# Graph attention on one core: vector engine and DMAs turn ten heads of twelve, values one graph later

## The reference

```python
q, k, v = (split_heads(x @ W + b) for W, b in ((Wq, bq), (Wk, bk), (Wv, bv)))
scores = einsum('bhqd,bhkd->bhqk', q, k) / sqrt(32) + beta * adj
probs = softmax(where(adj > 0, scores, -9e15))
x = layernorm(x + merge_heads(einsum('bhqk,bhkd->bhqd', probs, v)))
```

## Time and profile before

| | before |
|---|---|
| median of 3 runs | 678.68 us |
| the profiled execution, its own time | 678.75 us |
| its span, first to last instruction | 677.0 us |
| PE busy | 635.4 us, 94% |
| PE weight loads busy | 514.5 us, 76% |
| DVE busy | 597.7 us, 88% |
| ACT busy | 576.0 us, 85% |
| POOL busy | 406.9 us, 60% |
| DMA queue of SP | 100.37 MB, 57.9% of 16 engines |
| mean granted TensorE clock | 0.993 |

### The profile page before, as it was taken

The page is one execution under the profiler, slowest core; times in us unless marked ns, Lnnn a source line. Parts: engine busy times, 40 slices in busy tenths (PEclk is TensorE's granted clock), DMA queues, the critical chain, the costliest instruction groups (busy, mean ns, idle before and its releaser), DMA issues. The chain is left out here.

```text
span 677.0 us, 21340 instructions
## 1 busy us (share of the span) xinstructions
PE 635.4 (94%) x6304; PEld 514.5 (76%) x6304; DVE 597.7 (88%) x2385; ACT 576.0 (85%) x2024; POOL 406.9 (60%) x642
## 2 busy tenths in 40 slices
PE   5899999999999999999999999999999999999981
PEld 5788877787878787878777777888787878787850
DVE  3898899988999898989898989898989998898974
ACT  4799888889898889898888888888989888988881
POOL 3413266766566775566775556676556676566743
PEclk9999999999999999999999999999999999999997
DMA  8065556567656557755557755556765556765441
GB/s 254 4 148 142 139 136 166 126 164 187 172 143 162 137 140 189 185 150 153 145 122 187 187 155 151 153 119 177 188 172 144 154 127 157 189 168 144 114 101 70
DMA packets 68226, 101.93 MB, mean 151 GB/s; under 512 B 10512, under 2 KB 36368, under 8 KB 68112
## 3 DMA queue, kind: packets, MB, share of 16 engines
q1 hardware_dynamic: 67024, 100.37, 57.9%
q10 hardware_dynamic: 1088, 0.20, 0.2%
HBM read 22.94 MB, written 12.58 MB: 52 GB/s over the span
## 5 line engine op out<-in xcount | busy, mean ns | idle before, releaser
L433 ACT ACTIVATE probs<-neg_scores,neg_max 128x256 f32<-128x256 f32 x768 | 382.4, 504 | 4.4 <-DVE neg_max L515 2.9
L515 DVE CUSTOM_DVE_ANT_0 neg_scores<-s_bank,bias_sb 128x256 f32<-128x256 f32 x768 | 282.3, 416 | 54.2 <-ACT probs L433 45.0
L554 DVE STREAM_TRANSPOSE blocks<-probs 128x512 f32<-128x512 f32 x248 | 171.3, 700 | 0.0
L433 ACT ACTIVATION_READ_ACCUMULATOR probs<-neg_scores,neg_max 128x1 f32 x768 | 149.8, 195 | 0.0
L326 PE MATMUL j_bank<-xt_high,w_high 128*128 128x256 f32 x576 | 115.6, 309 | 1.9 <-ACT w_high L465 1.5
L399 PE MATMUL s_bank<-qk 32*128 32x256 f32 x1536 | 110.0, 399 | 5.4 <-DVE neg_max L515 3.7
L399 PEld LDWEIGHTS s_bank<-qk 32*128 32x128 f32 x1536 | 72.6, 184 | 46.7 <-ACT v_sb L452 28.1
L760 POOL TENSOR_SCALAR o_sb<-y_sb,rstd,shift 128x384 f32<-128x384 f32 x60 | 99.3, 1662 | 9.6 <-POOL shift L755 9.6
L326 PE MATMUL j_bank<-xt_high,w_low 128*128 128x256 f32 x576 | 99.5, 280 | 0.0
L326 PE MATMUL j_bank<-xt_low,w_high 128*128 128x256 f32 x576 | 99.2, 280 | 0.0
L369 PE MATMUL j_bank<-ident,probs 128*128 128x128 f32 x544 | 84.1, 278 | 13.9 <-issue 12.8
(11 more groups left out here) (56 smaller groups left out, 899.2 us busy)
## 6 DMA issues: line engine op xcount, KB each, us to landing
shuffled<-blocks SPq DMA_DIRECT2D x496, 128.0 KB, 3.1
x_sb<-in_x_dram SPq DMA_DIRECT2D x32, 384.0 KB, 3.3
out_dram<-o_sb SPq DMA_DIRECT2D x30, 384.0 KB, 4.3
adj_sb<-in_adj_dram SPq DMA_DIRECT2D x32, 256.0 KB, 3.7
out_dram<-o_sb SPq DMA_DIRECT2D x4, 192.0 KB, 2.1
blocks<-in_L_gnn_Wq_dram SPq DMA_DIRECT2D x1, 576.0 KB, 5.8
blocks<-in_L_gnn_Wk_dram SPq DMA_DIRECT2D x1, 576.0 KB, 8.2
blocks<-in_L_gnn_Wv_dram SPq DMA_DIRECT2D x1, 576.0 KB, 9.6
```

Of the source, the lines that this page charges most:

```text
L433: nc.scalar.activation(probs[:, (T * s + t) % (T * NX), :], neg_scores[:, (T * s + t) % (T * NH), :], ACT.Exp, bias=neg_max[:, n % 2, t, h ...
L515: nc.vector.tensor_tensor_reduce(neg_scores[:, (T * s + t) % (T * NH), :], s_bank[h % J][:, t * N:(t + 1) * N], bias_sb[:, n % 2, t, :], - ...
L554: nc.vector.transpose(blocks[:, n % 2, :, h, :, :].rearrange("p k t q -> p t k q"), probs[:, slot:slot + T, :].rearrange("p t (k q) -> p t ...
```

## The change

Heads 8 and 9 go the way of DVE and DMAs too (HV = 10), so that PE turns heads 10 and 11 only. Now each O needs the shuffle, so O 2 of a graph also moves one graph later, as O 0 and O 1 were. The DMAs remain 16 per graph, each a quarter larger. ACT takes K instead of DVE. The jobs are spread anew over the steps. Three buffers go, to make room: beta*adj is written over the adjacency, the residual sum over `att`, and the rings `probs` and `probs_t` shrink. The moments move from step 8 to step 10, `seed` from 9 to 11; on POOL `residual(n + 1)` goes ahead of `add_residual(n - 2)`; on SP `load_x` goes last. In the last graph all heads are still turned by PE; ten of them are put into the free half of `shuffled` once O 2 of graph 29 has read it.

```diff
-    NX = 6
+    NX = 5
-    HV = 8
+    HV = 10
-    NP = 8
+    NP = 4
@@ jobs_of, graphs 0 to 30 @@
                 0: (("O", 1, n - 2),),
-                1: (("K", 0, n + 1),),
+                1: (("X", 0, n + 2), ("K", 0, n + 1)),
                 2: (("G", 1, n - 2), ("Q", 0, n + 1)),
-                3: (("V", 0, n + 1),),
-                4: (("O", 2, n - 1),),
-                5: (("X", 0, n + 2), ("K", 1, n + 1)),
-                6: (("G", 2, n - 1), ("Q", 1, n + 1)),
-                7: (("X", 1, n + 2), ("Q", 2, n + 1)),
+                3: (("K", 1, n + 1),),
+                4: (("O", 2, n - 2),),
+                5: (("X", 1, n + 2), ("Q", 1, n + 1)),
+                6: (("G", 2, n - 2), ("Q", 2, n + 1)),
+                7: (("V", 0, n + 1),),
                 8: (("O", 0, n - 1),),
                 9: (("X", 2, n + 2), ("K", 2, n + 1)),
                 10: (("G", 0, n - 1),),
...
@@ jobs_of, the last graph @@
-                1: (("O", 2, n - 1),),
+                1: (("O", 2, n - 2),),
-                3: (("G", 2, n - 1),),
+                3: (("G", 2, n - 2),),
...
-                11: (("O", 1, n),),
+                11: (("O", 2, n - 1), ("O", 1, n)),
...
-    last_jobs = (("G", 1, B - 1), ("O", 2, B - 1), ("G", 2, B - 1))
+    last_jobs = (("G", 2, B - 2), ("G", 1, B - 1), ("O", 2, B - 1), ("G", 2, B - 1))
...
     def on_act(job):
-        return job[0] in "QVXO" or (job[0] == "T" and (job[2] < B - 1 or job[1] % 2 == 1))
+        return job[0] in "QKVXO" or (job[0] == "T" and (job[2] < B - 1 or job[1] % 2 == 1))
@@ place_of @@
+            if n == B - 1 and h < HV:
+                half = shuffled[:, n % 2, :, :, :, :, :].rearrange("p k a h t q -> p (k a h t q)")
+                return (half[:, h * T * N:(h + 1) * T * N].rearrange("p (k q) -> p k q", k=T), ("O", 2, n - 2))
@@ sync, shuffle @@
                 if n >= 2:
-                    wait_job(sp, ("O", 1, n - 2))
+                    wait_job(sp, ("O", 2, n - 2))
@@ sync, the loop @@
                 shuffle(n)
+                if n + 3 < B:
+                    load_adj(n + 3)
+                if n >= 3:
+                    store(n - 3)
                 if n + 4 < B:
                     load_x(n + 4)
-                if n + 3 < B:
-                    load_adj(n + 3)
-                if n >= 2:
-                    store(n - 2)
+            store(B - 4)
@@ scalar, before the loop @@
-            for h in range(2):
-                exps(h)
-            for job in second_jobs:
+            exps(0)
+            for job in second_jobs[:2]:
+                take(job)
+            exps(1)
+            for job in second_jobs[2:]:
                 take(job)
@@ vector, take G @@
-                    wait(dve, y_ready, n - 1)
+                    if n < B - 1:
+                        wait(dve, normed, T * (n - 1))
@@ vector, the loop @@
-                    if h == 8 and n >= 2:
+                    if h == 10 and n >= 2:
                         for t in range(T):
                             moments(n - 2, t)
                         gather_moments(n - 2)
-                    if h == 9 and n >= 2:
+                    if h == 11 and n >= 2:
                         seed(n - 2)
@@ gpsimd @@
             def bias(n):
-                pool.wait_ge(adj_in[n % 2], (n // 2 + 1) * DMA)
-                wait(pool, bias_ready, n)
-                take_wait()
-                nc.gpsimd.tensor_scalar(adj_beta[:, :, :], adj_sb[:, n % 2, :, :], 0.0, beta_col[:, 0:1],
+                pool.wait_ge(not_edge_ready, n + 1)
+                nc.gpsimd.tensor_scalar(adj_sb[:, n % 2, :, :], adj_sb[:, n % 2, :, :], 0.0, beta_col[:, 0:1],
                                         ALU.max, ALU.mult).then_inc(adj_beta_ready, 1)
...
             def add_residual(n):
                 pool.wait_ge(taken_v, max(dve_taken[place["G", g, n] + 1] for g in range(G)))
                 pool.wait_ge(res_ready, n + 1)
-                wait(pool, normed, T * n)
-                nc.gpsimd.tensor_tensor(y_sb[:, :, :], att[:, n % 2, :, :], x_sb[:, n % XB, :, :], ALU.add).then_inc(y_ready, 1)
+                nc.gpsimd.tensor_tensor(att[:, n % 2, :, :], att[:, n % 2, :, :], x_sb[:, n % XB, :, :], ALU.add).then_inc(y_ready, 1)
@@ gpsimd, the loop @@
                 if n + 1 < B:
                     bias(n + 1)
-                if n >= 2:
-                    add_residual(n - 2)
                 if n + 1 < B:
                     residual(n + 1)
                 if n >= 2:
+                    add_residual(n - 2)
                     layer_norm(n - 2)
```

More of the change, by code:

```diff
@@ L108, in on_act @@
     def on_act(job):
-        return job[0] in "QVXO" or (job[0] == "T" and (job[2] < B - 1 or job[1] % 2 == 1))
+        return job[0] in "QKVXO" or (job[0] == "T" and (job[2] < B - 1 or job[1] % 2 == 1))
     def on_dve(job):
-        return job[0] in "KXG" or (job[0] == "T" and not on_act(job))
+        return job[0] in "XG" or (job[0] == "T" and not on_act(job))
     act_taken, dve_taken = [0], [0]
@@ L443, in take @@
                 if kind == "T":
[L444 to L447, removed]
+                    copy, left = place_of(n, a)
+                    if left:
+                        wait_job(act, left)
+                    ins = nc.scalar.activation(copy, b[:, :].rearrange("p (k q) -> p k q", k=T),
                                                ACT.Identity)
-                elif kind == "Q":
-                    ins = nc.scalar.activation(qk[:, n % 2, 0, a, :], b[:, 0:N], ACT.Identity, bias=qk_bias[:, 0, a:a + 1])
+                elif kind in "QK":
+                    q = "QK".index(kind)
+                    ins = nc.scalar.activation(qk[:, n % 2, q, a, :], b[:, 0:N], ACT.Identity, bias=qk_bias[:, q, a:a + 1])
                 elif kind == "V":
@@ L497, in _ @@
                 act.wait_ge(out_done[n % 2], DMA * (B // 2 - 1))
-                nc.scalar.activation(o_sb[:, n % 2, 1, :], att[:, n % 2, 1, :], ACT.Identity, scale=last_rstd[:, T * i + 1:T * i + 2],
+                nc.scalar.activation(o_sb[:, n % 2, 1, :], att_of(n)[:, 1, :], ACT.Identity, scale=last_rstd[:, T * i + 1:T * i + 2],
                                      bias=last_shift[:, T * i + 1:T * i + 2]).then_inc(last_normed_a, 1)
@@ L526, in take @@
                     wait_job(dve, job)
[L527 to L533, removed]
+                    copy, left = place_of(n, a)
+                    if left:
+                        wait_job(dve, left)
+                    ins = nc.vector.tensor_copy(copy, b[:, :].rearrange("p (k q) -> p k q", k=T))
                 elif kind == "X":
@@ L600, in norm_last @@
                     if i == 1:
-                        for job in last_jobs[1:]:
+                        for job in last_jobs[2:]:
                             take(job)
@@ L648, in _ @@
             weights_low(1)
-            for job in first_jobs[C:]:
-                take(job)
             maxima(0)
-            take(second_jobs[0])
-            maxima(1)
-            take(second_jobs[1])
             weights_low(2)
-            for s in range(2, J):
+            for s in range(1, J):
                 maxima(s)
-            for job in second_jobs[2:]:
+            for job in second_jobs:
                 take(job)
@@ L694, in _ @@
             invert(B - 1, G - 1)
-            take(last_jobs[0])
+            for job in last_jobs[:2]:
+                take(job)
             norm_last()
@@ L759, in layer_norm @@
                 for t in range(T):
-                    nc.gpsimd.tensor_scalar(o_sb[:, n % 2, t, :], y_sb[:, t, :], rstd[:, t:t + 1], shift[:, t:t + 1],
+                    nc.gpsimd.tensor_scalar(o_sb[:, n % 2, t, :], att[:, n % 2, t, :], rstd[:, t:t + 1], shift[:, t:t + 1],
                                             ALU.mult, ALU.subtract).then_inc(normed, 1)
```

36 lines of the change are left out of this document (21 added, 15 removed).

## The result

The changed kernel takes 702.6 us (four runs, 700.2 to 704.3) against 678.9: ratio 1.034, 95% interval 1.031 to 1.038. It is slower, where I had forecast 662.5. The profiled execution took 703.1 us with a span of 701.3.

The account below looks back on a forecast made before the run. PE bound the kernel before; after the change the shuffle's closed loop would, at 19.5 us per graph: 678.75 - 17.6 (28 graphs against 20.13) + 1.5 at the end = 662.6, given as 662.5 us, range 645 to 678.

Parts of the forecast that it names:

- the engines' sums: Busy time per graph after the edits: PE 18.60, DVE 18.46, ACT 17.98 us; POOL's instructions the same.
- The loop: Shuffle, O 0, next graph's first scores, maxima, turn of head 9, next shuffle: 5.0 us on engines, period 19.5 us.
- POOL's chain: From head 9's block turn through moments, Newton steps, biases and residual sum: 19.0 us, 19.45 with SP's load issue.
- the length of the shuffle: Sixteen DMAs, a quarter larger: 12.1 us at share 0.94 plus 1.7, then 0.7 for the load of x: 14.5 us.
- at SP's pace: Undisturbed shuffle of graph 0: 16 DMAs issued at 0.685 us each, 12.7 us in all, against 0.57 engine time each.
- now have their place after the shuffle: Argument against a slower shuffle: the three tensors of loads and stores formerly around it come after it.
- Rival (b): Shuffle late at O 0 in step 8, deciding from 15.1 us; at 16 us period 21.0, time 704.6; chance 0.10.
- its formula: Late shuffle: period is its length plus 5.0 us; time is 678.75 plus 28 graphs' excess over 20.13, plus 1.5.
- the row of least disturbance: Shuffle of graph 0, 12.7 us in all; the forecast took 13.8 as nearest to it, from a span up to 17.1.
- The bound behind it: If the shuffle hides, PE and DVE bound at a period of 18.9 us: 645.8 us in all, chance 0.25.
- At the start: Start of the kernel, where ACT now makes the first K: between -1 and +1 us, taken as 0.
- The rule on the DMA engines: SBUF-to-SBUF transfers at 435 GB/s would make the quarter free; the forecast followed the profile row, full at 230 GB/s.

## Why the prediction was wrong

**What bounds before, and the engines' sums: nearly right.** DVE is at 18.54 us per graph (18.46 forecast), ACT at 17.98 (17.98). PE fell by 0.70 us to 18.92 and not by 1.02 to 18.60; 0.15 of the difference lies in the three graphs at the lower clock, since without them (the run with POOL's sum first) it is 18.77. The shorter ring `probs` and the in-place sums cost nothing that the run with HV = 8 shows; the ring `probs_t` had its old length there and was not tested.

**The loop: right in its parts.** Its turn on the engines was forecast as 5.0 us with SP's start and PE's answer; from O 0's start to the next shuffle it is 4.8. POOL's chain was forecast as 19.0 us from the former block turn to the issue of the load of x; that issue comes after 19.3 us (19.1 to 19.6), and after 19.1 in the run with fewer bytes.

**The step that failed: the length of the shuffle.** I put it at 14.5 us, 14.7 to O 0's start; it is 15.9. The mechanism was the right one, a term of its sum was too small. I had 12.1 us for the packets and 0.7 for the load of x ahead of them, from 0.57 us of engine time per DMA, a quarter added, and a share of 0.94. By the packet records of the 25 steady graphs they take 13.4 us, with all 16 engines busy throughout (0.99). Of these 13.4 the shuffle's own packets are 11.8 us of the engines' time, 0.74 per DMA and not 0.71. The load of x has 0.06 us of its packets among them in the mean. But the load of the adjacency, which is issued right behind the sixteenth DMA, has 1.0 us of its packets mixed into the shuffle's last 1.5 us: my argument that the other transfers "now have their place after the shuffle" holds for their issues and not for their packets, as the issues end some 10.9 us after the first began and the packets only after 14.8. No run moved that load. The rest is at the end: from the last packet to O 0 are 1.1 us, of which my sum had some 0.6; why it is longer than before (0.4 us to the landing, now 0.9) stays open.

The shuffle of before was at SP's pace, as I had called it: its packets take 11.0 us, with the engines busy 0.87 of that. The quarter and the load behind it used up that reserve and cost 2.4 us of packets and not 1.1. With 15.9 instead of 14.7 the loop asks for 15.9 + 4.8 = 20.7, above the 19.8 at which POOL's chain and the load of x come in, and the median graph has 20.64.

**Rival (b) was it,** a shuffle late at O 0 by itself; I gave it 0.10, its threshold as 15.1 us and its time at 16 us as 704.6. The landing comes after 15.7 us, for which its formula gives 678.75 + 28 x 0.54 + 1.5 = 695; the three long graphs bring most of the other 7 us. My count was 0.6 us from that threshold, on a term taken from the row of least disturbance. Nearness to a threshold should have been in the chance, as it was in no number. The range also ended at 678, where the loop's own length at the threshold is.

**The bound behind it was wrong too.** I had 18.9 us for PE and DVE alone. With the loop slack the runs show 19.6 (fewer bytes), 20.0, 20.3 and 19.8 us, by the order of the jobs. Busy sums of 18.8 and 18.5 us did not give a period of 18.9. My reading is that the two hand over to each other three times per graph and each stretch costs the larger of the two; one run bears it out, in which jobs moved between the stretches took the period from 20.3 to 19.8. Even with the shuffle free I should have said 670, not 646.

**At the start** I took 0; the loop also holds the first three graphs, which had been shorter, at 20 us and more: +4.0 us, and 1.6 for the later first shuffle. At the end I took +1.5; it is -0.2.

**The rule on the DMA engines** (the Trainium skill, DMA: Bandwidth & Descriptors, section Bandwidth) gives transfers within SBUF the fabric's 435 GB/s. The changed kernel's window inside the shuffle shows 224 GB/s at 0.98 busy; with that rule as I had used it the larger shuffle would have been hidden, and it was not. The same section of the Trainium skill makes that figure up from 16 ports of SBUF. Each DMA of the shuffle runs from 32 partitions to 32, and no run here shows how many ports these reach, so what binds at 224 GB/s stays open.

## What to carry to other kernels

Before moving work from a busy engine to a queue, look for what the queue's landing now stands in front of: if an in-order engine waits for the landing ahead of work that leads to the next issue, transfer and work add up to a period, and no engine is busy all of it. Price such a loop before the engines, with the whole way from first issue to the consumer's start as the trace has it. If the share of the DMA engines is near 0.9, scale the packets' part of it by the bytes (11.0 us x 1.25 = 13.8 here; it took 13.4), and count the packets of what is issued right behind. What helped here is the order: let the waiting job stand behind everything that leads to the next transfer, and then balance the stretches between handovers, not the sums.

## What the hardware showed that I had not expected

A wait of about 2 us of PE in the loop cost more than itself: the three graphs with waits of 1.97, 2.05 and 2.25 us took 22.9 to 23.2 us instead of 20.6, each with a stretch at a granted clock of 0.50 right behind the wait; no other steady graph of that trace, with waits up to 1.6 us, has one. Block DMAs within SBUF with 2.5 KB per packet moved 196 GB/s over a whole shuffle, and 224 in a window inside it at 0.98 busy, where loads and stores show 345. The load issued right behind the shuffle had its packets among the shuffle's last. And moving the load of x from 1 to 3 us ahead of the shuffle did not shorten its packets (13.5 against 13.4 us); it only took away the long waits.
